# The second feed-forward bias: from a matmul product per tile to an add on GpSimd

## The chip, the core and the metric

The kernel runs on one core of one Trainium2 chip. Its time is the device time of that core in microseconds (us). Three runs of the kernel before gave a median of 693.61 us (693.23 to 693.93).

A core has five engines that run side by side and meet only at semaphores: TensorE (PE: matrix products, with its weight loads as PEld), VectorE (DVE), ScalarE (ACT), GpSimd (POOL), and SyncE (SP), which here does nothing but issue DMAs. Every engine takes its own instructions strictly in order, so whatever stands behind a waiting instruction waits too.

## The reference

A transformer layer over 4 sequences of 2048 rows of 256 values, in float32: a layer norm, windowed causal attention with 16 heads of 16 and a window of 64 keys, its output product and a residual; then a layer norm, a feed-forward part with ternary weights, and a second residual.

```python
x = hidden                                   # [4, 2048, 256]
n = layernorm(x)
q, k, v = heads(n @ Wq.T), heads(n @ Wk.T), heads(n @ Wv.T)
a = softmax(q @ k.T / 4 + local_causal_bias) @ v      # window of 64 keys
x = x + merge(a) @ Wo.T
n = layernorm(x)
h = relu(n @ ternary(W1).T + b1)             # 1024 wide
x = x + (h @ ternary(W2).T + b2)             # b2: 256 values, the same for every row
```

## The kernel before, in words

The 8192 rows are worked in 16 chunks of 512 rows. One list of *slots* n sets the order on every engine: SLOTS runs from -44 to 303, each engine loops over it and emits in slot n whatever the position tables at the head of the file say. Scores of chunk c stand in slots 16c to 16c+15, one group of queries in each. Around them:

- Stage A prepares chunk c during the 16 slots ahead: layer norm, transposes, Q, K and V products. TensorE's V products stand at positions 10 and 13; VectorE finishes the second V half (`vd`, line 792) at position 14.
- SyncE then spreads the results: `place_v` (line 304, 16 DMAs into `vb`), `place_q` (line 284, 8 or 12 DMAs into `qbd` and `qm`), `place_k` (lines 263 to 268, into `k` and `kw`). In the steady part the order of its queue from the second V half on is: 16 of V, 8 of the second half of Q, 2 of the second half of K (`k` of head groups 2 and 3). The scores of position 8 (line 980, preceded by the mask product of line 973 or 969) are the first to read that K.
- The softmax runs through all engines: TensorE scores `ps` (980), VectorE row maximum `negm` (724), ScalarE exponentials `p` (523), VectorE turn `pt` (741), GpSimd the fp16 high and low parts `th` and `tl` (`low`, 417 and 419, one pair in every slot, three slots behind the scores), TensorE the products with V (1000, in every fourth slot).
- ScalarE and VectorE add the halves of the attention output into `osum`; GpSimd divides it (`o_norm`, 391, positions 13 and 5) and splits it into fp16 parts `oTh` and `oTl` (`o_split`, 397 and 399, positions 15 and 7).
- Stage C finishes chunk c in the 16 to 32 slots after: the output product `wo` (1062, positions 8 and 11), the first residual on VectorE (806), statistics (813 to 822), GpSimd's `rstd_c` and `c_norm` (384 to 407, positions 12 and 16, into `xnC`), transposes `c_t` (1074, positions 12 and 17), the first feed-forward product `c_f` (1089), the second `c_y` (1096 to 1101, positions 18, 19 and 25, 26), and the second residual (806, positions 20 and 27). Positions above 15 lie in the next chunk's slots: 18 is 2 of the next, 25 is 9 of the next. `wo` at position 8 waits for the `o_split` at position 7 (semaphore s_ol).

The residual rows stay in SBUF, in `xs`, from the load of the input to the store of the output. `c_y` opens its sum in PSUM with a product of a tile of ones with `bp[:, F:]`, which holds b2 as an fp16 part in row 0 and an fp16 rest in row 32, all other rows zero; the sixteen products of the hidden tile with W2 follow. The first bias b1 sits in `bp[:, 0:F]` and is folded into W1 at the start.

## Time and profile before

| | us |
|---|---|
| median of 3 runs (lowest, highest) | 693.61 (693.23, 693.93) |
| the profiled execution | 696.39 |
| its span in the trace | 694.6 |
| time outside the span | 1.79 |
| TensorE matmul busy | 653.9 (94%) |
| TensorE weight loads busy | 557.4 (80%) |
| VectorE busy | 611.0 (88%) |
| ScalarE busy | 567.7 (82%) |
| GpSimd busy | 556.4 (80%) |

The profiled execution took 2.78 us more than the median of the runs, and 1.79 us of its time lie outside the span. All rows further down are from this execution. Busy time of matmuls is modelled, since matmuls are pipelined: the distance from one start to the next says more of what a product takes than its duration. The granted TensorE clock was 0.98 of full speed over the span.

### The profile page before, as it was taken

The numbers are of one execution on the slowest core, as the hardware profiler recorded it, in microseconds if no ns is written. First come the engines' busy times: TensorE is split into PE (matmuls) and PEld (weight loads), VectorE is DVE, ScalarE is ACT, GpSimd is POOL, SyncE is SP. The second block draws the span as 40 slices with busy tenths as digits, with TensorE's granted clock in tenths as the row PEclk, the third lists the DMA queues.
The fourth block names the chain that finished last, engine by engine and source line by source line (L and its number), as shares of the span: only waits on it lengthen the run. The fifth ranks groups of instructions, "written<-read, shape, count | busy, mean of one in ns | idle before, by whom it ended". The sixth has DMA issues, their size and how long they took to land.

```text
span 694.6 us, 23901 instructions
## 1 busy us (share of the span) xinstructions
PE 653.9 (94%) x8048; PEld 557.4 (80%) x8048; DVE 611.0 (88%) x1391; ACT 567.7 (82%) x2489; POOL 556.4 (80%) x823
## 2 busy tenths in 40 slices
PE   7668789999999999999999999999999999998888
PEld 5446578888888888888878898888888888887776
DVE  4879889898999989899998999899899989897854
ACT  5588788898998988898988988898898988796622
POOL 7367899888888979888887989888898978887831
PEclk9889899999999999999999999999999999999999
DMA  8555563746465654736465564746465463643110
GB/s 291 77 104 114 90 111 62 142 81 114 78 130 96 132 98 92 134 78 118 85 132 96 115 117 90 123 82 122 85 131 98 90 114 58 122 81 78 32 39 31
DMA packets 314433, 70.59 MB, mean 102 GB/s; under 512 B 283076, under 2 KB 305862, under 8 KB 314312
## 3 DMA queue, kind: packets, MB, share of 16 engines
q1 hardware_dynamic: 281848, 42.43, 38.7%
q10 hardware_dynamic: 32464, 26.63, 13.2%
q8 instruction: 65, 1.06, 0.7%
q14 instruction: 56, 0.46, 0.2%
HBM read 20.25 MB, written 9.44 MB: 43 GB/s over the span
## 4 chain that ended last, share of the span: by engine, by line
PE 69%; SPq 7%; POOL 6%; DVE 6%; DMA 5%; ACT 4%; issue 3%; ACTq 0%; POOLq 0%; DVEq 0%
PE ps L1101 14%; PE ps L1089 11%; PE ps L1000 10%; PE ps L980 9%; PE ps L1037 8%; PE ps L1062 6%; PE ps L1048 4%; SPq L284 4%; DMA k<-kst 3%; SPq L304 3%; POOL tl L419 2%; PE ps L973 2%; PE ps L1074 2%; ACT p L523 2%; PE ps L1026 2%
## 5 line engine op out<-in xcount | busy, mean ns | idle before, releaser
L523 ACT ACTIVATE p<-ps,negm 128x96 f32<-128x96 f32 x1024 | 335.0, 355 | 16.9 <-DVE negm L724 16.3
L419 POOL TENSOR_TENSOR tl<-pt,th 128x384 f16<-128x384 f32 x256 | 234.4, 916 | 20.7
L523 ACT ACTIVATION_READ_ACCUMULATOR p<-ps,negm 128x1 f32 x1024 | 228.1, 223 | 0.0
L724 DVE TENSOR_REDUCE negm<-ps 128x4 f32<-128x384 f32 x256 | 138.2, 540 | 39.3 <-PE ps L980 36.3
L417 POOL CAST th<-pt 128x384 f16<-128x384 f32 x256 | 128.8, 503 | 32.0 <-DVE pt L741 31.8
L741 DVE STREAM_TRANSPOSE pt<-p 128x384 f32<-128x384 f32 x256 | 143.5, 561 | 3.0 <-ACT p L523 2.9
L980 PE MATMUL ps<-k,qbd 128*128 128x96 f16 x1536 | 125.6, 207 | 0.0
L980 PEld LDWEIGHTS ps<-k,qbd 128*128 128x128 f16 x1536 | 106.1, 99 | 11.1 <-issue 0.3
L1000 PE MATMUL ps<-th,vb 128*128 128x96 f16 (+1 forms) x1120 | 100.5, 205 | 2.2 <-DVE osum L800 1.6
L1000 PE MATMUL ps<-tl,vb 128*128 128x96 f16 (+1 forms) x1120 | 100.5, 205 | 0.0
L1000 PEld LDWEIGHTS ps<-th,vb 128*128 128x128 f16 x1120 | 96.4, 115 | 2.8 <-issue 1.7
L1089 PE MATMUL ps<-xTCh,w1T 128*128 128x256 f16 x512 | 97.6, 272 | 0.8 <-ACT xTCh L571 0.8
L1000 PEld LDWEIGHTS ps<-tl,vb 128*128 128x128 f16 x1120 | 95.8, 115 | 0.0
L576 ACT ACTIVATE hTh<-ps 128x512 f16<-128x512 f32 x128 | 78.6, 614 | 16.8 <-PE ps L1089 16.3
L833 DVE SCALAR_TENSOR_TENSOR hTl<-ps,hTh 128x512 f16<-128x512 f32 x128 | 86.9, 680 | 3.0 <-ACT hTh L576 3.0
L1089 PE MATMUL ps<-xTCl,w1T 128*128 128x256 f16 x256 | 69.8, 273 | 1.2 <-DVE xTCl L826 1.2
L1089 PE MATMUL ps<-xTCl,w1L 128*128 128x256 f16 x256 | 69.8, 273 | 0.0
L1101 PE MATMUL ps<-w2T,hTl 128*128 128x256 f16 x512 | 66.5, 273 | 0.2 <-DVE hTl L833 0.2
L1101 PE MATMUL ps<-w2T,hTh 128*128 128x256 f16 x512 | 66.4, 273 | 0.0
L980 PE MATMUL ps<-kw,qm 128*128 128x96 f16 x512 | 61.3, 211 | 0.0
L391 POOL TENSOR_TENSOR osum<-osum,rwide 128x512 f32<-128x512 f32 x32 | 40.6, 1268 | 22.1 <-DVE osum L800 21.4
L567 ACT ACTIVATE ohalf<-ps 64x512 f32<-64x512 f32 x64 | 38.0, 594 | 23.6 <-PE ps L1000 21.2
(141 smaller groups left out, 1430.7 us busy)
## 6 DMA issues: line engine op xcount, KB each, us to landing
k<-kst SPq DMA_DIRECT2D x32, 288.0 KB, 4.0
vb<-vd SPq DMA_DIRECT2D x256, 32.0 KB, 2.0
rwide<-parked ACTq DMA_DIRECT2D x32, 256.0 KB
out<-x ACTq DMA_DIRECT2D x32, 256.0 KB, 3.7
qbd<-qs SPq DMA_DIRECT2D x254, 32.0 KB, 2.8
x<-in_L_attn_hidden ACTq DMA_DIRECT2D x15, 512.0 KB, 4.5
kw<-kst SPq DMA_DIRECT2D x31, 192.0 KB, 4.4
k<-kst SPq DMA_DIRECT2D x31, 144.0 KB, 3.8
```

The lines of the kernel that those rows point to most:

```text
L417: e.tensor_copy(th[g % 2][:, o], pt[n % 3][:, :]).then_inc(s_hp, 1)
L419: e.tensor_tensor(tl[g % 2][:, o], pt[n % 3][:, :], th[g % 2][:, o], ALU.subtract).then_inc(s_lo, 1)
L523: ins = e.activation(p[:, 96 * u:96 * u + 96], bank[:, 96 * u:96 * u + 96], ACT.Exp, bias=m[:, u:u + 1], accum_out=r[:, u:u + 1])
L576: e.activation(hT[0][:, 2 * f:2 * f + 2, :].rearrange("p a b -> p (a b)"), c_bank(c, f"f{h}{f}")[:, :], ACT.Relu).then_inc(s_chi, 1)
L724: e.tensor_reduce(negm[n % 4][:, :], sbank[n % 3][:, 0:384].rearrange("p (a b) -> p a b", b=96), AX.X, ALU.max, negate=True).then_inc(s_mx, 1)
L741: e.transpose(pt[n % 3][:, :], pr[n % NP][:, :]).then_inc(s_tr, 1)
L833: e.scalar_tensor_tensor(out=lo, in0=c_bank(c, f"f{h}{f}")[:, :], scalar=0.0, in1=hi, op0=ALU.max, op1=ALU.subtract).then_inc(s_cdv, 1)
L980: ins = e.matmul(bank[:, 96 * u:96 * u + 96], to[:, g % 2, 128 * blk:128 * blk + 128], keys, start=(g < 2 and not first and m == 0 and u = ...
L1000: ins = e.matmul(pvbank[:, 32 * i0:32 * i1], lhs, rhs, start=(k == k0 and tt is th), stop=(k == 15), skip_group_check=True)
L1037: ins = e.matmul(bank[:, :], wT[n][wp][:, k, 128 * t:128 * t + 128], xTA[xp][:, k, :], start=(m == 0), stop=(m == 5))
L1089: ins = e.matmul(bank[:, o], w, xTC[xp][:, k, :], start=(xp + k == 0), stop=(xp + k == 2))
L1101: ins = e.matmul(bank[:, o], hT[hp][:, f, t * 128:(t + 1) * 128], w2T[:, f, :], start=False, stop=(f == 7 and hp == 1))
```

## The change

b2 is loaded with one DMA onto all 128 partitions of a new tile `b2w`. A new function `add_b2` on GpSimd adds it in place to two row tiles (128 x 512 float32) of `xs`, at positions 14 and 18 (C_B2), after the `low` of that slot and after the `c_norm` that reads the same rows. `c_y` no longer has its product of ones, and its first product opens the sum. The second residual waits for the add (semaphore s_b2). The fp16 parts of b2 with their memset, cast and subtraction in the start-up are gone, and `bp` holds b1 alone.

```diff
--- before.py
+++ after.py
@@ -24,6 +24,7 @@
 N_STATS, N_RSTD, N_NORM = ((-14, 1, 11), (-13, 2, 17)), (-12, 3, 21), ((-5, 7, 23), (-3, 9, 22))
 Q_DMA, K_DMA, V_DMA, A_CARRY = (7, 20), (15, 22), 17, 1
 C_WO, C_STATS, C_RSTD = (8, 11), (10, 14), (12, 16)
+C_B2 = (14, 18)
 C_T, C_F, C_Y = (12, 17), (14, 20), (18, 25)
 OUT_DMA, X_DMA = (23, 29), 36
 X_LATE = (8, 17, 25)
@@ -147,7 +148,7 @@
 
         fold = [sb(f"fold{i}", [128, 128], f16) for i in range(4)]
         identh = sb("identh", [128, 128], f16)
-        bp = sb("bp", [128, F + D], f16)
+        bp = sb("bp", [128, F], f16)
         xs = [sb(f"x{i}", [128, 4, D], f32) for i in range(NX)]
         xnA = sb("xnA", [128, 4, D], f32)
         xnC = sb("xnC", [128, 2, D], f32)
@@ -187,6 +188,7 @@
         ohalf = sb("ohalf", [64, CH], f32)
         oT = [sb(f"oT{p}", [128, 2, CH], f16) for p in "hl"]
         hT = [sb(f"hT{p}", [128, 8, CH // 2], f16) for p in "hl"]
+        b2w = sb("b2w", [128, 1, D], f32)
         gpart = sb("gpart", [128, 2, 2], f32)
         gsum = sb("gsum", [128, 2], f32)
         thr = sb("thr", [128, 2], f32)
@@ -215,7 +217,7 @@
         s_stA, s_agA, s_mvA, s_xnA = sem("s_stA"), sem("s_agA"), sem("s_mvA"), sem("s_xnA")
         s_stC, s_agC, s_mvC, s_xnC = sem("s_stC"), sem("s_agC"), sem("s_mvC"), sem("s_xnC")
         s_const, s_wlo, s_fc = sem("s_const"), sem("s_wlo"), sem("s_fc")
-        s_xn0 = sem("s_xn0")
+        s_xn0, s_b2, d_b2 = sem("s_xn0"), sem("s_b2"), sem("d_b2")
         s_gs, s_thr, s_tb, s_td = sem("s_gs"), sem("s_thr"), sem("s_tb"), sem("s_td")
 
         s_fe = sem("s_fe")
@@ -234,7 +236,7 @@
         junk = [hT[i // 2][:, 4 * (i % 2):4 * (i % 2) + 4, :].rearrange("p a b -> p (a b)") for i in range(4)]
         n1, n2 = n1.rearrange("p (a b) -> p a b", b=256), n2.rearrange("p (a b) -> p a b", b=1024)
         smask, kmask = pr[0][:, 0:64].bitcast(f16), pr[0][:, 64:112].bitcast(f16)
-        bt = (hT[0][:, :, :].rearrange("p a b -> p (a b)").bitcast(f32), hT[1][:, 0:2, :].rearrange("p a b -> p (a b)").bitcast(f32))
+        bt = hT[0][:, :, :].rearrange("p a b -> p (a b)").bitcast(f32)
         below = hT[1][:, 4:8, :].rearrange("p a b -> p (a b)").bitcast(f32)
 
         def a_bank(c, w):
@@ -315,8 +317,8 @@
             e.dma_start(pr[1][:, :], maskf_d).then_inc(d_m, 16)
             e.wait_ge(s_bz, 1)
             for r in (0, 32):
-                e.dma_start(bt[0][r:r + 1, :], b1_d.rearrange("(a n) -> a n", a=1)).then_inc(d_b, 16)
-                e.dma_start(bt[1][r:r + 1, :], b2_d.rearrange("(a n) -> a n", a=1)).then_inc(d_b, 16)
+                e.dma_start(bt[r:r + 1, :], b1_d.rearrange("(a n) -> a n", a=1)).then_inc(d_b, 16)
+            e.dma_start(b2w[:, 0, :], b2_d.rearrange("(a n) -> a n", a=1).to_broadcast([128, D])).then_inc(d_b2, 16)
             e.dma_start(n1, w1_d.rearrange("(t p) d -> p t d", p=128)).then_inc(d_w["1"], 16)
             e.dma_start(n2, w2_d.rearrange("(t p) f -> p t f", p=128)).then_inc(d_w["2"], 16)
             for n in SLOTS:
@@ -335,8 +337,7 @@
         @block.gpsimd
         def _(e):
             def clear_keys_and_queries():
-                e.memset(bt[0][:, :], 0.0)
-                e.memset(bt[1][:, :], 0.0).then_inc(s_bz, 1)
+                e.memset(bt[:, :], 0.0).then_inc(s_bz, 1)
                 for t in range(2):
                     ins = e.memset(kst[0][t][:, :, 0:64], 0.0)
                 ins.then_inc(s_zk, 1)
@@ -363,9 +364,8 @@
                     ins.then_inc(s_zv, 1)
 
             def biases():
-                e.wait_ge(d_b, 64)
-                e.tensor_copy(bp[:, 0:F], bt[0][:, :])
-                e.tensor_copy(bp[:, F:], bt[1][:, :]).then_inc(s_bh, 1)
+                e.wait_ge(d_b, 32)
+                e.tensor_copy(bp[:, :], bt[:, :]).then_inc(s_bh, 1)
 
             def rstd_a(c):
                 m = c % 2
@@ -407,6 +407,14 @@
                     ins = e.tensor_scalar(xnC[:, t, 0:D - 1], xs[c % NX][:, 2 * u + t, 0:D - 1], rstdC[u][:, t:t + 1],
                                           shiftC[u][:, t:t + 1], ALU.mult, ALU.add)
                 ins.then_inc(s_xnC, 1)
+
+            def add_b2(h):
+                c, u = divmod(h, 2)
+                e.wait_ge(s_xnC, h + 1)
+                if h == 0:
+                    e.wait_ge(d_b2, 16)
+                x2 = xs[c % NX][:, 2 * u:2 * u + 2, :]
+                e.tensor_tensor(x2, x2, b2w[:, :, :].to_broadcast([128, 2, D]), ALU.add).then_inc(s_b2, 1)
 
             def low(n):
                 g = n // 4
@@ -448,6 +456,10 @@
                     clear_values(2, m)
                 if 0 <= n - L_PART < NQ:
                     low(n - L_PART)
+                for u in range(2):
+                    c = stage_c(n, C_B2[u])
+                    if c is not None:
+                        add_b2(2 * c + u)
                 ct = pair_at(n, R_MUL)
                 if ct is not None:
                     o_norm(*ct)
@@ -687,8 +699,7 @@
 
             def bias_low():
                 e.wait_ge(s_bh, 1)
-                e.tensor_tensor(bp[32:64, 0:F], bt[0][32:64, :], bp[32:64, 0:F], ALU.subtract)
-                e.tensor_tensor(bp[32:64, F:], bt[1][32:64, :], bp[32:64, F:], ALU.subtract).then_inc(s_bias, 1)
+                e.tensor_tensor(bp[32:64, :], bt[32:64, :], bp[32:64, :], ALU.subtract).then_inc(s_bias, 1)
 
             def sums():
                 e.wait_ge(s_abs, 4)
@@ -803,6 +814,8 @@
             def residual(c, u, name):
                 x2 = xs[c % NX][:, 2 * u:2 * u + 2, :].rearrange("p a b -> p (a b)")
                 e.wait_ge(s_c, USE[c, name] + 1)
+                if name[0] == "y":
+                    e.wait_ge(s_b2, 2 * c + u + 1)
                 e.scalar_tensor_tensor(out=x2, in0=c_bank(c, name)[:, :], scalar=1 / WS if name[0] == "w" else 1.0,
                                        in1=x2, op0=ALU.mult, op1=ALU.add).then_inc(s_cdv, 1)
 
@@ -1093,13 +1106,12 @@
             def c_y(c, h, t):
                 bank = free("C", c, f"y{h}")
                 o = slice(t * 256, (t + 1) * 256)
-                e.matmul(bank[:, o], ones[:, 0:128], bp[:, F:], start=True, stop=False)
                 for hp, done, count in ((0, s_chi, SPLIT), (1, s_cdv, USE)):
                     for f in range(8):
                         if f % 2 == 0:
                             e.wait_ge(done, count[c, f"f{h}{f // 2}"] + 1)
                         ins = e.matmul(bank[:, o], hT[hp][:, f, t * 128:(t + 1) * 128], w2T[:, f, :],
-                                       start=False, stop=(f == 7 and hp == 1))
+                                       start=(f == 0 and hp == 0), stop=(f == 7 and hp == 1))
                 if t:
                     ins.then_inc(s_c, 1)
 
```

Places where rows move. GpSimd, positions 13 to 16 of a chunk (osum is `o_norm`, oTh and oTl `o_split`, xnC `c_norm`, th and tl `low`), before:

```order
L391 TENSOR_TENSOR osum<-osum,rwide 128x512
L417 CAST th<-pt 128x384
L419 TENSOR_TENSOR tl<-pt,th 128x384
L417 CAST th<-pt 128x384
L419 TENSOR_TENSOR tl<-pt,th 128x384
L397 CAST oTh<-osum 128x512
L399 TENSOR_TENSOR oTl<-osum,oTh 128x512
L384 TENSOR_TENSOR rstdC<-veC,mhalf 128x2
L386 TENSOR_TENSOR shiftC<-meanC,rstdC 128x2
```

and after:

```order
L391 TENSOR_TENSOR osum<-osum,rwide 128x512
L425 CAST th<-pt 128x384
L427 TENSOR_TENSOR tl<-pt,th 128x384
L417 TENSOR_TENSOR x<-x,b2w 128x512
L425 CAST th<-pt 128x384
L427 TENSOR_TENSOR tl<-pt,th 128x384
L397 CAST oTh<-osum 128x512
L399 TENSOR_TENSOR oTl<-osum,oTh 128x512
L384 TENSOR_TENSOR rstdC<-veC,mhalf 128x2
L386 TENSOR_TENSOR shiftC<-meanC,rstdC 128x2
```

The add (x<-x,b2w) stands between the `low` of position 14 and that of position 15; nothing else moved here. GpSimd again, positions 1 to 4, from the carried keys (kst) to the norm of stage A (rstdA), before:

```order
L358 COPY kst<-kst 128x2x64 x2
L417 CAST th<-pt 128x384
L419 TENSOR_TENSOR tl<-pt,th 128x384
L417 CAST th<-pt 128x384
L419 TENSOR_TENSOR tl<-pt,th 128x384
L417 CAST th<-pt 128x384
L419 TENSOR_TENSOR tl<-pt,th 128x384
L375 TENSOR_TENSOR rstdA<-veA,mhalf 128x4
```

and after:

```order
L359 COPY kst<-kst 128x2x64 x2
L425 CAST th<-pt 128x384
L427 TENSOR_TENSOR tl<-pt,th 128x384
L425 CAST th<-pt 128x384
L427 TENSOR_TENSOR tl<-pt,th 128x384
L417 TENSOR_TENSOR x<-x,b2w 128x512
L425 CAST th<-pt 128x384
L427 TENSOR_TENSOR tl<-pt,th 128x384
L375 TENSOR_TENSOR rstdA<-veA,mhalf 128x4
```

The second add stands behind the `low` of position 2. TensorE, positions 9 and 10 (ps<-bp,ones is the product with b2, w2T the second feed-forward product), before:

```order
L973 MATMUL ps<-maskf,identb 128x4x2x32
L980 MATMUL ps<-k,qbd 128x96 x8
L1096 MATMUL ps<-bp,ones 128x256
L1101 MATMUL ps<-w2T,hTh 128x256 x8
L1101 MATMUL ps<-w2T,hTl 128x256 x8
L973 MATMUL ps<-maskf,identb 128x4x2x32
L980 MATMUL ps<-k,qbd 128x96 x8
L1096 MATMUL ps<-bp,ones 128x256
L1101 MATMUL ps<-w2T,hTh 128x256 x8
L1101 MATMUL ps<-w2T,hTl 128x256 x8
```

and after:

```order
L986 MATMUL ps<-maskf,identb 128x4x2x32
L993 MATMUL ps<-k,qbd 128x96 x8
L1113 MATMUL ps<-w2T,hTh 128x256 x8
L1113 MATMUL ps<-w2T,hTl 128x256 x8
L986 MATMUL ps<-maskf,identb 128x4x2x32
L993 MATMUL ps<-k,qbd 128x96 x8
L1113 MATMUL ps<-w2T,hTh 128x256 x8
L1113 MATMUL ps<-w2T,hTl 128x256 x8
```

One product is gone from the head of each `c_y`.

## Rows read from the trace of the kernel before

**Rows 1.** The page: busy time of the engines, and the chain by engine.
```profile
PE 653.9 (94%) x8048; PEld 557.4 (80%) x8048; DVE 611.0 (88%) x1391; ACT 567.7 (82%) x2489; POOL 556.4 (80%) x823
...
PE 69%; SPq 7%; POOL 6%; DVE 6%; DMA 5%; ACT 4%; issue 3%; ACTq 0%; POOLq 0%; DVEq 0%
```

**Rows 2.** Groups by line: out<-in, shape, count | busy us, mean ns | idle before.
```profile
L1096 PE MATMUL ps<-bp,ones 128*128 128x256 f16 x64 | 17.5, 274 | 0.0
```

**Rows 3.** Timeline of TensorE from 307 us: start, duration, instruction.
```profile
307.19 0.28 PE L1096 MATMUL ps<-bp,ones 128*128 128x256 f16 x1
307.30 1.04 PE L1101 MATMUL ps<-w2T,hTh 128*128 128x256 f16 x8
```

**Rows 4.** Timeline of SyncE's DMA issues, 336 to 361 us.
```profile
337.71 11.66 SPq L304 DMA_DIRECT2D vb<-vd  x16
349.47 7.11 SPq L284 DMA_DIRECT2D qbd<-qs  x8
356.70 1.48 SPq L263 DMA_DIRECT2D k<-kst  x2
```

**Rows 5.** Timeline of VectorE at 337 us.
```profile
337.01 0.67 DVE L792 SCALAR_TENSOR_TENSOR vd<-ps,vd 128x512 f16<-128x512 f32 x1
```

**Rows 6.** The chain that ended last, 318 to 362 us: start, duration, what.
```profile
320.95 0.34 PE ps L980 x8
...
356.70 4.03 DMA k<-kst
...
361.19 0.34 PE ps L980 x8
```

**Rows 7.** Timeline of GpSimd, 303 to 321 us; idle time before in brackets.
```profile
303.25 1.13 POOL L407 TENSOR_SCALAR xnC<-x,rstdC,shiftC 128x255 f32<-128x255 f32 x2
...
311.25 1.01 POOL L375 TENSOR_TENSOR rstdA<-veA,mhalf 128x4 f32<-128x4 f32 x1 [0.61 <-DVE veA L767]
...
315.57 1.27 POOL L391 TENSOR_TENSOR osum<-osum,rwide 128x512 f32<-128x512 f32 x1 [0.15 <-DVE osum L800]
316.78 0.51 POOL L417 CAST th<-pt 128x384 f16<-128x384 f32 x1
...
320.36 1.16 POOL L399 TENSOR_TENSOR oTl<-osum,oTh 128x512 f16<-128x512 f32 x1
```

**Rows 8.** Timeline of GpSimd: the split of position 7 in two more chunks.
```profile
124.52 1.17 POOL L399 TENSOR_TENSOR oTl<-osum,oTh 128x512 f16<-128x512 f32 x1
...
359.35 1.15 POOL L399 TENSOR_TENSOR oTl<-osum,oTh 128x512 f16<-128x512 f32 x1
```

**Rows 9.** Timeline of TensorE: output products of position 8, one transpose of position 17.
```profile
126.72 0.38 PE L1062 MATMUL ps<-woh,oTh 128*128 128x256 f16 x2
...
305.97 0.60 PE L1074 MATMUL ps<-identf,xnC 128*128 128x128 f32 x4
...
322.58 0.38 PE L1062 MATMUL ps<-woh,oTh 128*128 128x256 f16 x2
...
362.68 0.38 PE L1062 MATMUL ps<-woh,oTh 128*128 128x256 f16 x2
```

**Rows 10.** Timeline of GpSimd, 650 to 662 us.
```profile
655.76 1.13 POOL L407 TENSOR_SCALAR xnC<-x,rstdC,shiftC 128x255 f32<-128x255 f32 x2
...
660.29 0.91 POOL L419 TENSOR_TENSOR tl<-pt,th 128x384 f16<-128x384 f32 x1
```

**Rows 11.** Timeline of TensorE at 657 us.
```profile
656.94 0.66 PE L1074 MATMUL ps<-identf,xnC 128*128 128x128 f32 x4 [1.73 <-POOL xnC L407]
```

**Rows 12.** The chain that ended last, from 590 us.
```profile
634.66 2.34 PE ps L1000 x36
...
661.30 1.60 PE ps L1000 x36
...
687.38 0.11 PE ps L1096
```

**Rows 13.** Busy time by stretch (PE, PEld, DVE, ACT, POOL), granted clock, DMA.
```profile
600.00:640.00 40.00, 37.04 (x481) 32.66 (x480) 32.87 (x72) 30.33 (x146) 32.22 (x47) 0.96 0.47 88
```

## The prediction

> **What bounds the kernel now.** The page comes first. TensorE's matmuls are busy 94% of the span, the others 80 to 88%, and the chain of waits lies on TensorE for 69% [rows 1]. Taken alone this says that TensorE is the bound and that every product removed is time won. The Trainium skill ("Trainium Kernel Development and Optimization", Performance Expectations) warns of just that number: matmul busy time is a bad measure, because matmuls are pipelined. What the sum would be by the 94% stands among the rivals as the 7.0 us case.
>
> So the second thing to look at is what releases TensorE, chunk by chunk. In the chain each stretch of TensorE work in the steady part ends at the scores of position 8, which start just after the K of head groups 2 and 3 has landed. The DMA row starts at 356.70 and lasts 4.03, so it lands at 360.73, and the scores run from 361.19; one chunk earlier they started at 320.95 [rows 6]. Follow the loop between these two starts. VectorE finishes the second V half at 337.01 + 0.67 = 337.68 [rows 5], 16.73 after the scores. SyncE issues its first V DMA at 337.71, needs 11.76 for sixteen of them and 7.23 for eight of Q, and issues K at 356.70 without a pause [rows 4]. Then 4.03 for the transfer and 0.46 to the scores. 16.73 + 0.03 + 18.99 + 4.03 + 0.46 = 40.24, the whole distance. So the steady part is a loop of two pieces: TensorE and VectorE own it from position 8 to 14, SyncE's queue and one transfer own it from position 14 to the next position 8. In the second piece TensorE is busy all the while, but some tenths ahead of what the loop asks for, and waits them out before position 8. I take it for the loop of every chunk from the second on: read in the same way, the landings of the other chunks stand the same few tenths before their scores.
>
> GpSimd is third. It runs from about position 14 to position 8 of the next chunk nearly without a pause: the only idle times that the timeline brackets there are 0.61 before the norm of stage A and 0.15 before `o_norm` [rows 7]. It is not the bound, but its backlog ends in `o_split`, and the output product of position 8 waits for that.
>
> **The change part by part.**
>
> *Products removed.* 64 products [rows 2]. What one costs is the distance to the next start, 307.30 - 307.19 = 0.11, not its 0.28 [rows 3]. 32 of them, at positions 18 and 19, lie in SyncE's piece of the loop (positions 2 and 3 of the next chunk): TensorE gets 0.22 further ahead and waits it out. They are worth nothing in the steady part. The other 32, at positions 25 and 26 (9 and 10), lie in TensorE's piece: 0.22 a chunk. Over the 13 passages of the loop that follow, 13 x 0.22 = 2.8 us won. In the tail the chain runs through the last products one after the other, as at 687.38 [rows 12]; eight of ones are left there, two of them behind a GpSimd result that comes late anyway (below), so 6 x 0.11 = 0.66 won.
>
> *Adds.* 32 instructions on GpSimd, 128 x 512 float32 with two inputs in SBUF. The nearest row is `o_norm`, same shape and types: 1.27 long, but the next instruction starts 316.78 - 315.57 = 1.21 after it [rows 7]. I take 1.21. The lower end is `oTl`, the same elements with a 2-byte operand and output: 1.16 long [rows 7], 1.10 if it too reaches 0.06 into the next. The broadcast operand has no row; I let it go up to 1.45, an estimate, a fifth above `o_norm`. The Trainium skill ("Perfetto Trace Analysis", GPSIMD Engine Instruction) says that a GpSimd span in a profile is not to be trusted and that the start-to-start distance should be used. The trace bears it out: the 1.27 reaches 0.06 into the next row. By spans the two adds would be 2.54 a chunk in place of 2.42, and the sum below 0.9 us more.
>
> *What the adds push.* Both stand inside the backlog: position 14 is two slots before `c_norm` of position 16, position 18 is position 2. Nothing is idle between them. Behind them in GpSimd's queue are, in order: `low` of position 15, the first `o_split`, `c_norm`, the carried keys, `low` after `low`, `o_norm`, the second `o_split`. Their readers have different room:
> - the transposes of position 17: 305.97 - (303.25 + 1.13) = 1.59 after their operand [rows 7, 9]. Only the first add (1.21) is ahead of them. No wait, with 0.3 left.
> - `low` feeds VectorE's turn and the products with V, two slots or more behind; 2.4 late fits.
> - the output product of position 8. The second split ends at 320.36 + 1.16 = 321.52 and the product starts at 322.58: room 1.06 [rows 7, 9]. It is 1.03 in the first steady chunk (126.72 against 124.52 + 1.17) and 2.18 at its widest (362.68 against 359.35 + 1.15) [rows 8, 9].
>
> For this last one: 2.42 of adds, less the idle time that absorbs them. The brackets give 0.76; small gaps that are not bracketed add a little, I take 0.85. Late by 1.57, against the room less 0.05 for the signal. Over the 13 chunks of the loop the room is 1.02 to 1.06 in four, 1.26 and 1.34 in two, 1.58 and more in seven. So 4 x 0.57 + 2 x 0.32 = 2.9 us of new waits. They lie in TensorE's piece of the loop, just behind position 8, so they count in full: everything that VectorE and SyncE do later in the loop comes later too. The 2.8 won in that same piece are given back.
>
> *Start-up.* Up to the first steady output product, at 126.72, GpSimd itself is the backlog and nothing there is idle: 2.42 - (1.03 - 0.05) = 1.4 us lost. The products removed so far lie in waits.
>
> *Tail.* In the last chunk's slots GpSimd is on the path itself: TensorE is idle 1.73 until `xnC`, which ends at 655.76 + 1.13, and starts at 656.94 [rows 10, 11]. The first add of chunk 14 stands before it: +1.2. The same add makes the last `tl` late (ends 660.29 + 0.91 = 661.20, read from 661.30 [rows 10, 12]), which is why the two products removed between them give nothing. The last two adds fall into idle time of GpSimd.
>
> *The rest, at nothing.* The memset, cast and subtraction of b2 in the start-up run while those engines wait for loads. One DMA of b2 to 128 partitions (128 KB) takes the place of two small ones, ahead of the W1 and W2 loads; its reader comes only with the first stage C; 0 to 0.4 us if it delays W1, I take 0.1. The second residual waits for an add six or nine positions earlier. The semaphore on which `add_b2` waits is GpSimd's own and two slots old.
>
> Sum: -2.8 + 2.9 + 1.4 + 1.2 - 0.66 + 0.1 = +2.1 us. Against the profiled execution, a span of 694.6 and 1.79 outside it: 696.39 + 2.1 = 698.5. That execution was 2.78 above the median of the runs, so the time is 693.61 + 2.1 = 695.7.
>
> **The rivals.**
>
> *GpSimd's adds are hidden (not slower).* If the backlog is shorter than the margins say, because its inputs come earlier once TensorE has 0.22 more in hand, or the waits at position 8 move with the K landing (the wide rooms are those of chunks in which K landed late), the output product never waits. Place: position 8; it decides from a lateness under 1.0 us at the split. Then -2.8 - 0.66 + 0.5 in start-up and tail: 693.61 - 3.0 = 690.6. For it: 7 of 13 chunks have the room already. Against it: nothing absorbs the 2.42 but 0.85.
>
> *Half of both.* An add at 1.10 shortens each lateness by 0.2: waits 6 x 0.2 less, start-up 0.2, tail 0.1: 694.2, no change that can be told.
>
> *TensorE is the bound after all.* 64 x 0.11 = 7.0: 686.6. For it the 94% [rows 1]; against it the loop that closes to 40.24 through SyncE.
>
> *GpSimd overflows.* An add of 1.45 brings 0.48 more lateness at each split: waits in about nine chunks, 9 x 0.48 = 4, start-up 0.5, and 0.2 in the tail: 700. Part of it is that longer TensorE pauses lower its clock: at 634 us it had waited for K, and then the 36 products with V took 2.34 against 1.60 later, in a stretch with granted clock 0.96 [rows 12, 13]. A pause of 3 us before 657, where 1.73 is now, may do the same and cost 1 us.
>
> *It does not do what it says*: the second residual waiting for the add would show at positions 20 and 27; the order excludes it nearly.
>
> **How the numbers follow.** Forecast (+0.6 to +4 us) 0.45; hidden 0.17; half of both 0.22; TensorE the bound 0.04; overflow 0.12. Differences under 0.2%, 1.4 us, can't be told from no change. Faster (under 692.2) is the hidden case and TensorE: 0.21. Same (692.2 to 695.0) is half of both and the lower end of the forecast: 0.30. Slower 0.49. The range runs from the hidden case, 690.3, to 699.0, which leaves out TensorE as the bound and the top of the overflow. The likeliest case alone has 694.2 to 697.6.
>
> **What would show it.** Right: new idle time of TensorE before the output product, released by `oTl`, in four to seven chunks, of 0.3 to 0.7 us; K landing still just before the scores of position 8 in every chunk; GpSimd with almost no idle time from position 14 to 8; `x<-x,b2w` 1.2 from start to start; TensorE's wait for `xnC` near 657 grown to about 3. Wrong: no wait on `oTl` and a shorter distance between position-8 scores (hidden); new waits of VectorE's turn or of the position-17 transposes on GpSimd (overflow); waits for K gone (TensorE the bound).

## The result and the profile after

| | before | after |
|---|---|---|
| median of 5 runs each, us | 693.23 | 697.51 |
| lowest, highest | 689.33, 693.93 | 697.20, 699.80 |
| profiled execution (span) | 696.39 (694.6) | 697.20 (695.4) |
| TensorE matmul busy | 653.9 (94%) | 644.2 (93%) |
| GpSimd busy | 556.4 (80%) | 593.9 (85%) |

Ratio after to before 1.0088 [1.0052, 1.0125]: 3.6 to 8.7 us slower, where +2.1 was forecast. Run a second time, the changed kernel gave 1.0099 [1.0080, 1.0118]. Direction and place were right; the size was not.

From the page after, the busy times and the shares of the chain of waits, the answer to [rows 1]:

```profile
PE 644.2 (93%) x7984; PEld 546.0 (79%) x7984; DVE 611.0 (88%) x1390; ACT 567.7 (82%) x2489; POOL 593.9 (85%) x853
POOL 41%; PE 35%; DVE 9%; issue 7%; ACT 3%; SPq 2%; DMA 2%; POOLq 1%; DVEq 0%
```

TensorE has 64 instructions fewer and 9.7 us less to do, VectorE is where it was. The second row is the finding: the chain of waits has left TensorE and SyncE's queue and lies on GpSimd for 41% of the span, on an engine that is idle for 15% of it.

The adds and, of the same shape, `o_norm` (columns as in the page's table of groups: busy and mean ns, idle before and its releaser):

```profile
L417 POOL TENSOR_TENSOR x<-x,b2w 128x512 f32<-128x512 f32 x32 | 40.6, 1270 | 0.2
L391 POOL TENSOR_TENSOR osum<-osum,rwide 128x512 f32<-128x512 f32 x32 | 40.6, 1269 | 16.5 <-DVE osum L811 16.5
```

The broadcast operand costs nothing: an add is as long as `o_norm`, and from its start to the next one are 339.37 - 338.16 = 1.21, the price taken. The answers to [rows 7, 8] on GpSimd's timeline, one chunk later in the program, columns start, duration, instruction:

```profile
338.16 1.27 POOL L417 TENSOR_TENSOR x<-x,b2w 128x512 f32<-128x512 f32 x1
339.37 0.51 POOL L425 CAST th<-pt 128x384 f16<-128x384 f32 x1
...
349.62 1.27 POOL L417 TENSOR_TENSOR x<-x,b2w 128x512 f32<-128x512 f32 x1
...
352.33 1.01 POOL L375 TENSOR_TENSOR rstdA<-veA,mhalf 128x4 f32<-128x4 f32 x1
...
356.46 1.27 POOL L391 TENSOR_TENSOR osum<-osum,rwide 128x512 f32<-128x512 f32 x1
...
361.25 1.16 POOL L399 TENSOR_TENSOR oTl<-osum,oTh 128x512 f16<-128x512 f32 x1
```

The idle times that stood in brackets before stage A's norm (0.61) and `o_norm` (0.15) are gone: they absorbed part of the adds, as forecast. And TensorE at the output product of position 8 (line 1075 now), where [rows 9] had no bracket:

```profile
323.18 0.38 PE L1075 MATMUL ps<-woh,oTh 128*128 128x256 f16 x2 [0.20 <-POOL oTl L399]
...
362.55 0.38 PE L1075 MATMUL ps<-woh,oTh 128*128 128x256 f16 x2 [0.68 <-POOL oTl L399]
```

The split ends at 361.25 + 1.17 = 362.42 and the product starts 0.13 later. That is the forecast wait. It comes, however, in the first eleven of the thirteen steady chunks, not in six of them. The waits of TensorE after, whole span (us in total, times, longest):

```profile
PE ps L1075 <- POOL oTl L399: 8.7, 12, 1.7
PE ps L986 <- DMA k<-kst: 5.7, 4, 2.8
PE ps L1087 <- POOL xnC L407: 5.2, 3, 3.1
```

and of the unchanged kernel, run again:

```profile
PE ps L973 <- DMA k<-kst: 7.2, 8, 2.8
PE ps L1062 <- POOL oTl L399: 1.9, 2, 1.3
```

The chain of waits after, for one loop, shortened (start, duration, what):

```profile
323.18 1.47 PE ps L1075 x12
...
334.66 0.70 DVE osum L811
335.50 1.26 POOL osum L391
336.77 0.45 POOL th L425
337.30 0.91 POOL tl L427
338.21 1.23 POOL x L417
...
343.73 1.13 POOL xnC L407 x2
...
349.66 1.23 POOL x L417
...
352.36 0.98 POOL rstdA L375
...
361.25 1.17 POOL oTl L399
362.55 0.49 PE ps L1075 x3
```

Read it as a loop. From the output product of position 8 (323.18) TensorE, ScalarE and VectorE need 12.32 until `o_norm` starts on GpSimd (335.50). GpSimd then works 26.92 to the end of the late split (362.42), and 0.13 later comes the next output product: 12.32 + 26.92 + 0.13 = 39.37, the whole distance. SyncE and the K transfer don't occur in it. This is a **second loop** beside the one that the prediction followed through V, Q and K. Both share TensorE's part behind position 8, and the longer one sets the time of every chunk.

What was the loop before, [rows 4, 5], now. The second V half on VectorE's timeline:

```profile
337.39 0.67 DVE L803 SCALAR_TENSOR_TENSOR vd<-ps,vd 128x512 f16<-128x512 f32 x1
```

and SyncE's issues behind it, on SyncE's timeline:

```profile
338.09 11.26 SPq L306 DMA_DIRECT2D vb<-vd  x16
349.45 6.24 SPq L286 DMA_DIRECT2D qbd<-qs  x8
355.81 1.32 SPq L265 DMA_DIRECT2D k<-kst  x2
```

It still runs without a pause and still ends just before the scores of position 8 (360.06). The old loop hasn't vanished, it is stretched: TensorE's wait for the split lies in it too. From the scores of position 8 to the end of the second V half it now takes 17.20 on average over the thirteen steady chunks, and 17.19 in a second execution; with neither products nor adds it is 16.64.

### The profile page after: what moved, and what is told of

It reads as the page before. It is cut to its first block, busy times and chain, and to the rows that moved or that the text cites. A ratio compares the mean times of both kernels' runs of the same rounds, so it can differ in the third digit from the quotient of the medians.

```text
span 695.4 us, 23898 instructions
## 1 busy us (share of the span) xinstructions
PE 644.2 (93%) x7984; PEld 546.0 (79%) x7984; DVE 611.0 (88%) x1390; ACT 567.7 (82%) x2489; POOL 593.9 (85%) x853
## 3 DMA queue, kind: packets, MB, share of 16 engines
q1 hardware_dynamic: 281988, 42.56, 38.7%
q8 instruction: 65, 1.06, 0.7%
## 4 chain that ended last, share of the span: by engine, by line
POOL 41%; PE 35%; DVE 9%; issue 7%; ACT 3%; SPq 2%; DMA 2%; POOLq 1%; DVEq 0%
POOL tl L427 13%; PE ps L1113 10%; POOL th L425 7%; PE ps L1075 5%; POOL osum L391 4%; PE ps L1013 4%; PE ps L993 4%; POOL oTl L399 4%; POOL x L417 4%; PE ps L1102 3%; PE ps L1061 3%; PE ps L1050 3%; POOL xnC L407 2%; POOL oTh L397 2%; DVE negm L735 2%
## 5 line engine op out<-in xcount | busy, mean ns | idle before, releaser
L1013 PE MATMUL ps<-th,vb 128*128 128x96 f16 (+1 forms) x1120 | 98.5, 203 | 2.0 <-POOL tl L427 2.0
L1013 PE MATMUL ps<-tl,vb 128*128 128x96 f16 (+1 forms) x1120 | 98.5, 203 | 0.0
L1013 PEld LDWEIGHTS ps<-th,vb 128*128 128x128 f16 x1120 | 94.8, 114 | 2.3 <-POOL tl L427 2.2
L1013 PEld LDWEIGHTS ps<-tl,vb 128*128 128x128 f16 x1120 | 94.1, 114 | 0.0
L1113 PE MATMUL ps<-w2T,hTl 128*128 128x256 f16 x512 | 69.1, 275 | 0.8 <-DVE hTl L846 0.6
L1113 PEld LDWEIGHTS ps<-w2T,hTl 128*128 128x128 f16 x512 | 49.3, 99 | 10.1 <-DVE hTl L846 3.8
L391 POOL TENSOR_TENSOR osum<-osum,rwide 128x512 f32<-128x512 f32 x32 | 40.6, 1269 | 16.5 <-DVE osum L811 16.5
```

The costliest lines, as they stand in the source:

```text
L391: e.tensor_tensor(osum[:, t, :], osum[:, t, :], rwide[t][:, :], ALU.mult).then_inc(s_on, 1)
L1013: ins = e.matmul(pvbank[:, 32 * i0:32 * i1], lhs, rhs, start=(k == k0 and tt is th), stop=(k == 15), skip_group_check=True)
L1113: ins = e.matmul(bank[:, o], hT[hp][:, f, t * 128:(t + 1) * 128], w2T[:, f, :], start=(f == 0 and hp == 0), stop=(f == 7 and hp == 1))
```

## The experiments

Each ratio is to runs of the kernel before that were taken beside it: one set of them for the rows from "unchanged, again" to adds_17_25, a second for the next four, a third for adds_even, adds_384, adds_14_25 and "after, again". "Loop" is the distance from one output product of position 8 to the next, its two parts are "to `o_norm`" (from the product to the start of `o_norm`, position 13) and "GpSimd" (from there to the end of the late split). All are read from the timelines of the profiled executions, the parts as the mean of the first eleven of the thirteen steady loops, the loop as the lowest and the highest of the eleven (us).

| kernel | ratio to before [95%] | to `o_norm` | GpSimd | loop |
|---|---|---|---|---|
| before | | 12.53 | 25.26 | 38.7 to 40.1 |
| unchanged, again | 1.0008 [0.9983, 1.0032] | 12.53 | 25.26 | 38.5 to 39.7 |
| products_out | 0.9953 [0.9929, 0.9977] | 12.32 | 25.26 | 38.3 to 39.0 |
| adds_on_top | 1.0151 [1.0118, 1.0184] | 12.53 | 26.95 | 39.61 to 39.95 |
| adds_17_25 | 0.9968 [0.9944, 0.9991] | 12.32 | 25.68 | 38.2 to 39.1 |
| products_out_h0 | 0.9993 [0.9970, 1.0015] | 12.53 | 25.26 | 38.5 to 39.6 |
| products_out_h1 | 0.9955 [0.9936, 0.9974] | 12.32 | 25.26 | 38.5 to 39.7 |
| adds_narrow | 0.9978 [0.9962, 0.9995] | 12.32 | 25.80 | 38.2 to 39.1 |
| mixed | 0.9979 [0.9960, 0.9998] | 12.32 | 25.25 | 38.7 to 40.5 |
| adds_even | 1.0053 [1.0038, 1.0068] | 12.34 | 25.16 / 26.94 | 38.1 to 39.42 |
| adds_384 | 1.0049 [1.0030, 1.0069] | 12.32 | 26.38 | 38.80 to 40.2 |
| adds_14_25 | 0.9998 [0.9975, 1.0020] | 12.32 | 25.66 | 38.3 to 39.4 |
| after | 1.0088 [1.0052, 1.0125] | 12.31 | 26.93 | 39.37 to 39.43 |
| after, again | 1.0099 [1.0080, 1.0118] | 12.31 | 26.94 | 39.37 to 39.43 |

**The unchanged kernel again.**

> The kernel before, unchanged, for a second trace and for the size of the noise: the profiled execution of before was 2.8 us above the median of its runs. Ratio 1.000 within 0.2%. If the loop through SyncE bounds it, K lands just before the scores of position 8 in every chunk again, and what differs between two executions is where K lands and which stretches have half the TensorE clock.

Measured 692.12 against 691.94: what two sets of runs of one program differ by.

**Only the products gone, no adds.** b2 is left out of the result.

```diff
-                        add_b2(2 * c + u)
+                        pass
...
-                if name[0] == "y":
-                    e.wait_ge(s_b2, 2 * c + u + 1)
```

> The 64 products of ones are gone and nothing adds b2 in their place (b2 is left out of the output). Loop through SyncE: only the products of positions 25 and 26 and those of the tail count, -3.5 us (ratio 0.995). TensorE as the bound: -7.0 us (0.990). No output product waits for GpSimd.

Measured 688.40 against 691.94, -3.5 us (by the ratio -1.6 to -4.9). So the products were worth about what their terms said (-2.8 - 0.66), not 7.0, and the adds cost all of the loss and this gain besides: 9.3 to 10.1 us as the difference of the ratios (0.9953 against 1.0088 and 1.0099). Its chain of waits goes through SyncE's queue again:

```profile
PE 57%; SPq 14%; POOL 8%; DVE 8%; DMA 5%; ACT 4%; issue 3%; ACTq 0%; POOLq 0%; DVEq 0%
```

**Adds made, products kept.** b2 is added twice.

```diff
+                e.matmul(bank[:, o], ones[:, 0:128], bp[:, 0:D], start=True, stop=False)
...
-                                       start=(f == 0 and hp == 0), stop=(f == 7 and hp == 1))
+                                       start=False, stop=(f == 7 and hp == 1))
```

> The 32 adds on GpSimd are there and the products of ones are kept too (they read 256 values of b1 in place of b2, so b2 is right and a part of b1 comes on top). Late split: TensorE reaches the output product 0.22 us later than without the products, so the new waits are 0.35 to 0.57 us in the chunks with a room of 1.0 to 1.3 us; with start-up and tail +4 to +6 us against before. If the adds only cost because the products are gone (TensorE running ahead), +1 us or less.

Measured 702.81 against 691.94, a ratio that is far above what was expected. The loop is 39.61 to 39.65 in ten of eleven, 0.23 above that of the changed kernel, and its first part is 0.21 longer, which is the two products per chunk at 0.11. The second loop thus holds TensorE's products as well. From the third chunk's scores of position 8 to the last's it takes 514.1, against 509.2 and 507.9 before: 5.5 of the 10.4 us. Behind the loop, from the last chunk's scores of position 8 to the end, it takes 61.7 against 60.4, another 1.3. The profiled execution was 2.1 us below this kernel's median, and the rest has no place in its trace.

**The same adds at other positions.**

```diff
-C_B2 = (14, 18)
+C_B2 = (17, 25)
```

> The changed kernel with the adds at positions 17 and 25 in place of 14 and 18: one stands before the split of position 7, the other behind it, where GpSimd has idle time. Late split: one add of 1.21 less 0.85 of idle time is 0.36 late, under the room of 1.0, so no output product waits in the loop, and the tail loses the add before the last transposes: -2 to -3.5 us against before (0.996), 6 to 7 us under the changed kernel. If GpSimd's total load is the cost (85% busy), the place changes nothing and it stays at 1.009.

Measured 689.76 against 691.94. GpSimd does the same 32 adds, its busy time is unchanged, and the kernel is slightly faster than before, by 0.1 to 0.6%:

```profile
PE 642.2 (94%) x7984; PEld 546.1 (80%) x7984; DVE 607.6 (89%) x1390; ACT 567.3 (83%) x2489; POOL 593.7 (87%) x853
PE 65%; POOL 10%; SPq 7%; DVE 6%; DMA 4%; issue 4%; ACT 3%; ACTq 0%; POOLq 0%; DVEq 0%
```

On GpSimd's timeline the second add now stands behind the late split, with idle time ahead of the next `o_norm` to take it:

```profile
316.58 1.17 POOL L399 TENSOR_TENSOR oTl<-osum,oTh 128x512 f16<-128x512 f32 x1
320.60 1.27 POOL L417 TENSOR_TENSOR x<-x,b2w 128x512 f32<-128x512 f32 x1
...
331.01 1.27 POOL L391 TENSOR_TENSOR osum<-osum,rwide 128x512 f32<-128x512 f32 x1 [0.86 <-DVE osum L811]
```

Only one add is left in GpSimd's part, most of it absorbed: 25.68 against 25.26. 12.32 + 25.68 + 0.15 = 38.15 is shorter than the loop through SyncE, and the chain of waits shows K setting the pace again: it lands at 312.86 + 3.79 = 316.65, the scores run from 317.05.

```profile
312.12 0.63 SPq L286
312.86 3.79 DMA k<-kst
317.05 0.34 PE ps L993 x8
```

So it is the place of the adds, not GpSimd's load. Of the kernels here that compute everything this one has the lowest ratio.

**One half of the products gone at a time**, nothing else changed (those of positions 18 and 19 with `h != 0`, of 25 and 26 with `h != 1`); that half of b2 is left out.

```diff
-                e.matmul(bank[:, o], ones[:, 0:128], bp[:, F:], start=True, stop=False)
+                if h != 1:
+                    e.matmul(bank[:, o], ones[:, 0:128], bp[:, F:], start=True, stop=False)
```

> The kernel before without the 32 products of ones of positions 18 and 19 (b2 is left out of the first half of each chunk). They lie in SyncE's piece of the loop. Loop through SyncE: TensorE's piece (scores of position 8 to the end of the second V half) stays at 16.85 us, TensorE only waits longer for K, and the time moves by the tail alone, -0.4 us (ratio 0.9995). TensorE as the bound: half of -7.0 us (0.995).

> The kernel before without the 32 products of ones of positions 25 and 26 (b2 is left out of the second half of each chunk). They lie in TensorE's piece of the loop. Loop through SyncE: TensorE's piece goes from 16.85 to 16.64 us, 13 times, and with the tail -3.1 us (0.9955). TensorE as the bound: -3.5 us (0.995), the same as for positions 18 and 19.

The same 32 instructions: 0.9993 for those in SyncE's piece, 0.9955 for those in TensorE's. From the scores of position 8 to the end of the second V half the first kernel needs 16.86, like before, the second 16.65. The split of the 64 products into such as count and such as don't measurably is shown. The rival that TensorE is the bound has fallen with it: it asked 0.995 of the first kernel too, which lies outside the interval.

**Adds of half the width**, on one of the two row tiles; for the other b2 is left out.

```diff
-                x2 = xs[c % NX][:, 2 * u:2 * u + 2, :]
-                e.tensor_tensor(x2, x2, b2w[:, :, :].to_broadcast([128, 2, D]), ALU.add).then_inc(s_b2, 1)
+                x2 = xs[c % NX][:, 2 * u:2 * u + 1, :]
+                e.tensor_tensor(x2, x2, b2w[:, :, :], ALU.add).then_inc(s_b2, 1)
```

> The changed kernel with adds of half the width (one row tile of two; b2 is left out of the other). Two adds of some 0.65 us less 0.75 of idle time leave the split 0.55 late, under the smallest room of 1.0: no waits in the loop but in the start-up, so -2 to -3 us against before (0.996). If it is the number of adds or their waits that costs, not the time they take, it stays near the changed kernel (1.009).

0.9978: 12.32 + 25.80 + 0.15 = 38.27, still below the loop through SyncE.

**Adds of three quarters of the width** (192 of 256 columns of each tile; the rest of b2 left out).

```diff
-                x2 = xs[c % NX][:, 2 * u:2 * u + 2, :]
+                x2 = xs[c % NX][:, 2 * u:2 * u + 2, 0:192]
```

> The changed kernel with adds of 384 columns in place of 512 (b2 is left out of the rest), some 0.93 us each. The split is then 1.1 us late; against rooms of 0.84 to 1.84 us in the trace of the repeated kernel before, less 0.14 for the signal, TensorE waits in the four or five narrowest chunks only, 0.1 to 0.3 us each: loop -2.8 + 1.0, start-up +0.9, tail +0.3, so about -0.5 us against before (0.999). If the cost were proportional to the time of the adds it would lie midway between the half and the full width, 1.003.

A miss: 1.0049 where about 0.999 was expected. The second loop would be 12.32 + 26.38 + 0.15 = 38.85 here, and seven of the eleven loops lie between 38.80 and 38.88, so its length is as the sum says. The other four, up to 40.2, are longer, as the loop through K can be; the mean is 39.06, against 38.70 without adds and 39.39 with whole ones. Behind the loop, the tail is 62.0 against 60.4; TensorE's products are slowed by the lower clock at two places in it (the tail is taken up below). The profiled execution took 694.27, 2.3 us above the median of before (692.02), so about two thirds of the 3.4 us that the ratio gives are in this trace.

**Adds in every second chunk**; in the others b2 is left out.

```diff
-                    if c is not None:
+                    if c is not None and c % 2 == 0:
```

> The changed kernel with its two adds only in every second chunk (b2 is left out of the odd ones), so that no wait can stem from the one a chunk earlier. Theory without carry: each split behind adds is 1.67 us late and TensorE waits 0.5 to 0.6 us there, six times in the loop, and not in the other chunks; with start-up and tail as in the changed kernel about +2.5 us against before (1.003 to 1.005). Rival, carry (the wait of one chunk makes the next split later): the waits shrink to 0.3 us or less and the time is at or under that of before.

GpSimd's part alternates between 24.9 to 25.2 and 26.93 to 26.95, and the loop does too: 39.40 to 39.42 in all five chunks with adds (TensorE's waits for the split between 130 and 610 us are in the row below), 38.1 to 39.35 in the others. Nothing is carried from chunk to chunk.

```profile
PE ps L1075 <- POOL oTl L399: 3.1, 5, 0.8
```

The same row of the changed kernel is below; it names nine waits, and by the distance from split to product, 0.13 to 0.18 in all eleven chunks, TensorE waits in each of them. The shortest waits are not in the list.

```profile
PE ps L1075 <- POOL oTl L399: 4.9, 9, 0.9
```

**One add before the backlog's end, one behind the split.**

```diff
-C_B2 = (14, 18)
+C_B2 = (14, 25)
```

> The changed kernel with the second add at position 25 in place of 18, the first left at 14. In the loop like the adds at 17 and 25: one add before the split, lateness 0.4 us, no waits. In the tail the first add of chunk 14 still stands before the last transposes but one: +1.2 us of it, so -1 us against before (0.9985) and 1.2 us above the adds at 17 and 25.

0.9998 against 0.9968 for (17, 25), each against its own set of runs of before; the intervals overlap. The second loop is as short in both (GpSimd 25.66 and 25.68). The traces differ at the end: TensorE's wait for `xnC` is 3.12 here and 1.89 there, and the span behind the last chunk's scores of position 8 is 62.4 against 59.6. Of these 2.8 us, however, 1.6 have another origin. Right behind those scores TensorE ran at its lower clock here and not there: the 36 products with V and the 12 output products behind them took 1.92 + 2.45 here and 1.44 + 1.32 there, after waits for K of 3.42 and 2.80. That leaves 1.2 us, as long as one add, for what an add at position 14 costs outside the loop; one execution each carries it.

**Half and half, complete computation**: the product stays for positions 18 and 19, an add at position 25 serves the other two row tiles.

```diff
+C_B2 = 25
...
+                x2 = xs[c % NX][:, 2:4, :]
...
+                if h != 1:
+                    e.matmul(bank[:, o], ones[:, 0:128], bp[:, F:], start=True, stop=False)
```

> b2 in both ways: the first half of each chunk keeps its product of ones (positions 18, 19, in SyncE's piece), the second half gets an add on GpSimd at position 25, behind the split of position 7, and loses its products (25, 26). The whole computation is done. Loop through SyncE with a late split: no new wait and the gain of the loop's products, -3 us (0.9955), as good as the adds at 17 and 25 or better by their start-up wait. TensorE as the bound: -3.5 us (0.995); adds at 17 and 25, which remove twice as many products, would then be better than this by as much again.

0.9979 where 0.9955 was expected: faster than before by a hair, not distinguishable from (17, 25), and about half of the expected gain. Its trace has the shorter way to `o_norm` (12.32) and no longer GpSimd part (25.25). Yet its eleven loops take 39.22 on average, like before, because SyncE's piece, from the first V issue to the K landing, is 22.1 in this execution; it is the slowest of the twelve timed (694.99), so it says little of the median.

**The changed kernel again.**

> The changed kernel once more, beside the others on the same chip and for a second trace: 1.009 of before within 0.3%, TensorE's piece of the loop 17.2 to 17.3 us on average, a wait for the split in eleven or more chunks of the loop.

698.84 against 692.02. The loops, the wait for the split in eleven chunks and TensorE's piece (17.19) repeat those of the first execution.

## Why the prediction was right in kind and wrong in size

*The loop through SyncE, and the products.* Right. K lands some tenths before the scores of position 8 in nearly every chunk of all kernels, the products of positions 18 and 19 are worth nothing that can be measured, those of 25 and 26 are worth 0.21 a chunk where 0.22 stood. The sum -3.5 was measured as -3.5 in the medians. The profiled executions show more: from the third chunk to the last, 502.5 without products against 509.2 and 507.9. Part of it is that SyncE's own piece (V, Q and K) is 21.7 in that execution and 22.0 and 21.9 in the two before. In the four executions with products at positions 25 and 26 it is 21.9 or 22.0, in the ten without them 21.6 to 21.9 but for mixed (22.1); why is open.

*The adds.* 1.21 each, as forecast. No wait at the transposes of position 17, as forecast: their margin is 0.12 to 0.50, where 0.3 stood.

*The waits at position 8: the step that failed.* It read: "Over the 13 chunks of the loop the room is 1.02 to 1.06 in four, 1.26 and 1.34 in two, 1.58 and more in seven. So 4 x 0.57 + 2 x 0.32 = 2.9 us of new waits." The lateness was set against the room of each chunk, as if the room belonged to the chunk. It doesn't: in the unchanged kernel run again other chunks have the wide rooms, for a room is wide where K happened to be late. The wait ends when GpSimd's part ends, and that part starts from TensorE's work in the same loop: the loop through the split is closed, and its length is independent of the room. It was to be had from the trace of before by the same addition as the other one: 12.53 - 0.22 to `o_norm`, 25.26 + 2.42 of adds less what is absorbed, and the signal. Two small terms then count in each of eleven loops, not in six waits: the idle time absorbs 2.42 - (26.93 - 25.26) = 0.75, not 0.85, and from split to product are 0.15, not 0.05. Together 0.2 a loop.

*What is left of "2.8 won, 2.9 given back".* In the loop the changed kernel takes 511.1 and 511.2 from the third chunk to the last, 508.6 in the mean before, 502.5 without products and adds. Hence the adds cost some 8.6 there, not 2.9; 11 x (39.39 - 38.70), the mean loops with and without adds, is 7.6 of it. TensorE's piece says the same: 13 x (17.20 - 16.64) = 7.3 us of new waits. The gain of a shorter loop through SyncE, that unforeseen 0.2 a chunk included, is lost wholly once the other loop is the longer one.

*Start-up and tail.* The tail behind the last chunk's scores of position 8 is 60.8 after, against 60.4 in both executions before: +0.4, where 1.2 - 0.66 stood. That the number fits is luck: two effects outside the sum nearly cancel. TensorE's wait for `xnC` grew as said, 1.73 [rows 11] to 3.12:

```profile
656.94 0.67 PE L1087 MATMUL ps<-identf,xnC 128*128 128x128 f32 x4 [3.12 <-POOL xnC L407]
```

The 32 second feed-forward products behind it then ran partly at the lower clock, which they hadn't before; that cost 1.66 (5.15 against 3.49), and only the rival of the overflowing GpSimd named it. In return the stretch at the lower clock that stood 23 us earlier, behind the wait for K, is missing from the execution after. From the chain of waits, the products with V and the output products behind them, before:

```profile
634.66 2.34 PE ps L1000 x36
637.00 2.01 PE ps L1062 x12
```

and after:

```profile
635.07 1.44 PE ps L1013 x36
636.51 1.32 PE ps L1075 x12
```

The difference is 1.6 us, though TensorE had waited equally long for K, 2.80 before and 2.77 after. This stretch is there in nine of the fourteen profiled executions, both of before among them, and in neither of the two after; what decides it no run shows.

Of the start-up the traces don't decide: the first steady chunk comes at 124.9 and 123.2 in the two executions before, at 123.5 and 125.5 in the two after. The forecast of +1.4 is inside that spread. No run isolates the 0.1 for the DMA of b2.

With +2.6 in the loop and +0.4 in the tail, the profiled executions account for 3 of the 4.3 and 6.8 us by which the medians differ. The profiled executions before were 3.2 and 1.1 us above their medians, those after 0.3 below and 0.5 above. So the traces of before show slower executions than the typical one, and what is missing from the account lies there; the stretch behind the wait for K can be 1.6 us of it, which isn't shown.

*Two slips without effect.* The room at the output product is 2.69 at its widest (the last of the thirteen), not 2.18. And the range was said to begin at the hidden case with 690.3, which that case's own sum puts at 690.6.

*The rivals.* "The adds are hidden" fell for these positions and holds in the loop for (17, 25). Its idea that wide rooms go with late K landings was right, and spoke for the opposite conclusion. "TensorE is the bound" fell with the halves of the products. "Half of both" had the add too cheap (1.10). "GpSimd overflows" needed an add of 1.45; it is 1.21, and the time came near that case for another reason.

The Trainium skill ("SBUF — State Buffer", SBUF: two separate sides) says that VectorE and GpSimd share a pair of ports which one instruction holds to its end, and that a VectorE operation with two inputs in SBUF can thus block GpSimd. No row here shows it for the adds: their mean of 1270 ns is that of `o_norm` (1269), and VectorE's busy time is 611.0 both before and after. But no run sets out to test it, and `o_norm` could be held up in the same way.

## What to carry to other kernels

Where a steady pattern repeats, list all closed loops and add up the length of each, with the change in it: the period is that of the longest, and slack is the difference of two lengths, never the room that one execution happens to show in front of a wait. Terms of tenths then count once per period. Where two loops are nearly equal and one varies, the mean lies above both: 39.06 with the adds of three quarters, for 38.85 by one loop and 38.70 by the other. Work moved to an engine with idle time must go where that engine is idle within the loop: the same change cost 0.9% with its 32 adds at positions 14 and 18 and gained 0.3% with them at 17 and 25.

## What the runs showed of the hardware

- The loop through compute engines and semaphores alone is even here: 39.37 to 39.43 in eleven loops of each of two executions. The loop through SyncE's DMAs varies from 38.3 to 39.0 in one execution without the products and from 38.5 to 39.7 in one with them.
- SyncE's issues aren't alike. Those of one series in (17, 25), from its chain of waits:

```profile
307.67 0.64 SPq L286
308.35 0.69 SPq L286
309.08 1.64 SPq L286
310.76 0.63 SPq L286
```

  The fifth of the eight Q issues took 1.64 where the others take 0.6 to 0.7. In all fifteen chunks of this execution one of the eight is longer like this (0.95 to 1.96), most often the fifth. In the sixteen V issues too one stands out in each steady chunk, the fifth to the ninth (1.07 to 1.61). No run took it apart.
- After TensorE's pause of 3.12 the granted clock over the stretch around it is 0.76 (busy times with counts of PE, PEld, DVE, ACT, GpSimd, then the granted clock, DMA share, GB/s):

```profile
655.00:662.00 7.00, 5.06 (x31) 3.87 (x32) 1.81 (x3) 0.71 (x2) 6.57 (x11) 0.76 0.14 44
```

  It was at the lower of its two levels, 1.2 GHz, from 657.5 to 660.9. The 32 second feed-forward products took 5.15 there and 3.49 at the full clock 13 us later:

```profile
657.61 5.15 PE ps L1113 x32
670.49 3.49 PE ps L1113 x32
```

  The kernel with adds at (17, 25) shows the same 5.16 after a pause of 1.89. At this place all eight profiled executions with adds at two positions have such a stretch, after pauses of 1.89 to 3.13. The six others (before twice, products_out, its two halves, mixed) have none, after pauses of 1.72 to 1.77. Behind the wait for K the length of the pause doesn't tell them apart: no such stretch after 2.28, 2.77, 2.80, 2.81 and 2.99, and one after 2.76, 2.80, 2.92 and more.
